# Near heads of the second attention: products moved to POOL, weighted values moved into the attention stage, a skew of two batches, the gates' softmax in two halves

## The reference

```
qk = x @ Wqk + bqk                      # x: layernorm of the residual
q, k = split(qk);  v = k                # 16 heads of 16
windows = [max(4, 256 // 2 ** h) for h in range(16)]
mask = (j <= i) & (j > i - windows[h])
att = softmax(where(mask, q @ k.T / sqrt(16), -inf))
out = att @ v
gates = softmax(x @ Wgate + bgate)      # over the 16 heads
y = (out * gates) @ Wproj + bproj
```

## Time and profile before

| | us |
|---|---|
| three timed runs, median | 1461.62 |
| lowest, highest of them | 1457.1, 1462.15 |
| profiled execution, its own time | 1458.09 |
| its span in the profile | 1456.4 |
| busy in the span: PE, DVE | 1237.8, 850.5 |
| busy in the span: ACT, POOL | 660.5, 666.6 |
| `project_local`, from PE's first product to the end of the last row | 529.30 to 636.30 |
| `project_local`, from there to its last instruction | 636.30 to 665.64 |
| `attend`, SP's first load to DVE's last instruction | 666.15 to 805.21 |

### The profile page before, as it was taken

How to read it: one execution, slowest core, us unless ns; L and a number is a source line. 1 busy time by engine, 2 the same in 40 slices (tenths; PEclk the granted TensorE clock), 3 DMA queues, 4 the chain that set the end, 5 groups by cost and what they waited for, 6 DMA issues and landing times. The chain is left out here.

```text
span 1456.4 us, 29479 instructions
## 1 busy us (share of the span) xinstructions
PE 1237.8 (85%) x9695; PEld 969.9 (67%) x9696; DVE 850.5 (58%) x1794; ACT 660.5 (45%) x1260; POOL 666.6 (46%) x616
## 2 busy tenths in 40 slices
PE   5886999999978959944998786798869999999996
PEld 3664555555547747732766666788847888878885
DVE  4897788888738849985554684433323333333332
ACT  2881666666755534420445552233213433333332
POOL 6865777776351304876000000454224554444553
PEclk9996899999999968775999998999979999999998
DMA  2487999999300025654442420000174334554331
GB/s 54 141 277 248 259 285 270 274 275 286 69 1 1 1 82 162 195 159 91 111 110 51 144 73 8 18 26 30 37 285 133 57 60 127 134 133 131 56 50 20
DMA packets 122865, 179.26 MB, mean 123 GB/s; under 512 B 26052, under 2 KB 83820, under 8 KB 122772
## 3 DMA queue, kind: packets, MB, share of 16 engines
q1 hardware_dynamic: 105876, 159.62, 37.6%
q0 software_dynamic: 16896, 18.44, 7.5%
HBM read 104.73 MB, written 74.31 MB: 123 GB/s over the span
## 5 line engine op out<-in xcount | busy, mean ns | idle before, releaser
L1635 DVE TENSOR_REDUCE att_top<-att_psS 128x4 f32<-128x512 f32 (+2 forms) x192 | 195.0, 1037 | 45.2 <-PE att_psS L1522 42.2
L2786 POOL DMA_INDIRECT out<-ffn1c_y,ffn1c_table x72 | 113.4, 1575 | 180.4 <-ACT ffn1c_y L2899 112.3
L2927 DVE TENSOR_TENSOR ffn1c_hid<-ffn1c_psG,ffn1c_sil 128x512 f32<-128x512 f32 x72 | 49.8, 692 | 145.6 <-PE ffn1c_psG L2827 145.6
L1606 ACT ACTIVATE att_prob<-att_psS 128x1024 f32<-128x1024 f32 (+1 forms) x96 | 83.3, 887 | 63.0 <-PE att_psS L1536 63.0
L1516 PE MATMUL att_psS<-pairs_ka,pairs_qa 48*128 48x384 f32 (+3 forms) x512 | 100.0, 399 | 11.8 <-DMA pairs_ka<-k_parts 7.2
L2827 PE MATMUL ffn1c_psG<-ffn1c_w_h,ffn1c_xh 128*128 x288 | 98.0, 422 | 11.1 <-DMA ffn1c_w_l<-experts_lo 6.0
L2435 POOL DMA_INDIRECT slots<-ffn1b_entry,ffn1b_sloti x64 | 62.9, 983 | 92.1 <-ACT ffn1b_act_h L2648 52.6
L1606 ACT ACTIVATE pairs_part<-att_psS 128x1024 f32<-128x1024 f32 (+1 forms) x96 | 83.0, 889 | 35.8 <-PE att_psS L1536 35.8
L2775 POOL DMA_INDIRECT ffn1c_rows<-normed_rows,ffn1c_table x72 | 71.2, 988 | 46.6 <-DVE ffn1c_gate L2947 22.9
L2827 PE MATMUL ffn1c_psG<-ffn1c_w_l,ffn1c_xh 128*128 x288 | 91.4, 399 | 0.0
L2827 PE MATMUL ffn1c_psG<-ffn1c_w_h,ffn1c_xl 128*128 x288 | 91.1, 398 | 0.0
(11 more groups left out here) (397 smaller groups left out, 3518.4 us busy)
## 6 DMA issues: line engine op xcount, KB each, us to landing
prep_raw<-in_w_all SPq DMA_DIRECT2D x27, 512.0 KB, 5.6
experts_hi<-ffn0w_room SPq DMA_DIRECT2D x27, 512.0 KB, 5.9
experts_lo<-prep_lo SPq DMA_DIRECT2D x27, 512.0 KB, 7.4
ffn1c_w_h<-experts_hi SPq DMA_DIRECT2D x8, 1536.0 KB
ffn1c_w_l<-experts_lo SPq DMA_DIRECT2D x8, 1536.0 KB
qkv_near<-near_keys SPq DMA_DIRECT2D x32, 320.0 KB, 4.3
q_parts<-pairs_part SPq DMA_DIRECT2D x8, 1024.0 KB
k_parts<-pairs_part SPq DMA_DIRECT2D x16, 512.0 KB
```

The lines of the kernel that those rows point to most:

```text
L1606: act.activation(dst, src, ACT.Exp, scale=0.25).then_inc(s["exp"], 1)
L1635: dve.tensor_reduce(dst, src, AX.X, ALU.max).then_inc(s["max"], 1)
L2786: pool.indirect_dma_start(out=rows_out, in_=y[:, t.buf, :], in_offset=None, out_offset=bass.IndirectOffsetOnAxis(ap=table[:, t.value:t.val ...
L2927: dve.tensor_tensor(hid[:, t.par, :], psG[:, t.par, 1, :], sil[:, t.par, :], ALU.mult).then_inc(s["act"], 1)
```

## The change

In `project_local`:
- `near_products` goes from DVE to POOL, ahead of `third_term` in POOL's loop; of the last batch POOL makes two of the four planes and DVE the other two (`last_products`). `near` has two buffers and `qkr` three.
- The near work of batch b-2 stands in iteration b (before: b-1). `turn_rows` and `high_rows`/`low_rows` run two batches ahead (before: one), so two batches are turned before the first product. PE's order in an iteration is products, gate logits, `turn_wide` of b-1, `turn_rows` of b+2.
- The gates' softmax is made for four batches at once, at two places of the loop, instead of once for each batch. The near shares are no longer multiplied with the gates here.
- `near_values` is gone from here. The shares of all batches stay in SBUF (`near_shares`) for the next block.

In `attend`:
- SP reads the shifted keys again (`near_in`, two transfers of 320 KB in each unit's stage), and POOL multiplies shares with gates, keys with that, and adds the planes (`near_values`), once for each batch, behind its bias addition.
- The four constants are written by POOL, and PE waits for them only ahead of its first psB product.

```diff
@@ project_local, SP
                 sp.wait_ge(s["rows"], 16 * (b + 1))
-                if b >= 3:
-                    sp.wait_ge(s["pv1"], b - 2)
+                if b >= 2:
+                    sp.wait_ge(s["prod"], b - 1)
                 for d in range(NW):
...
@@ project_local, PE
             turn_rows(0)
+            turn_rows(1)
             pe.wait_ge(s["wt"], len(ws))
-            for b in range(B):
-                products(b)
-                if b + 1 < B:
-                    turn_rows(b + 1)
-                gate_logits(b)
-                turn_wide(b)
+            for b in range(B + 1):
+                if b < B:
+                    products(b)
+                    gate_logits(b)
+                if b >= 1:
+                    turn_wide(b - 1)
+                if b + 2 < B:
+                    turn_rows(b + 2)
...
@@ project_local, ACT
             high_rows(0)
             normed(1)
+            high_rows(1)
+            normed(2)
             act.wait_ge(s["ones"], 2)
...
+            for b in range(B + 1):
+                if b == B // 2 + 1:
+                    gate_exp(0)
+                if b < B:
+                    values(b)
                 if b >= 1:
-                    near_exp(b - 1)
-                gate_exp(b)
-                second_term(b)
+                    first_term(b - 1)
                 if b + 2 < B:
-                    normed(b + 2)
+                    high_rows(b + 2)
+                if b >= 2:
+                    near_exp(b - 2)
+                if b >= 1:
+                    second_term(b - 1)
+                if b + 3 < B:
+                    normed(b + 3)
+            gate_exp(1)
             near_exp(B - 1)
...
@@ project_local, POOL
+            def near_products(b, planes):
+                pool.wait_ge(s["qs"], TG * (b + 1))
+                pool.wait_ge(s_near[b % 2], 16 * NW * (b // 2 + 1))
                 if b >= 1:
...
+                    pool.wait_ge(s["sc0"], b)
+                pool.tensor_tensor(prod[:, 0:planes], near[:, b % 2, 0:planes],
+                                   qkr[:, b % 3, :, PW:D].unsqueeze(1).to_broadcast([P, planes, TG, DW]),
+                                   ALU.mult).then_inc(s["prod"], 1)
 
             for b in range(B):
-                pool.wait_ge(s["prod"], b + 1)
+                near_products(b, NW if b + 1 < B else NW // 2)
                 third_term(b)
-                if b >= 1:
-                    near_values(b - 1)
...
@@ project_local, DVE
             low_rows(0)
+            low_rows(1)
...
-            for n in range(B + 1):
+            for n in range(B + 2):
+                if n == B // 2:
+                    gate_logits(0)
                 if n < B:
                     rows(n, (0, 1))
-                if n >= 1:
-                    near_products(n - 1)
+                if n == B + 1:
+                    last_products(B - 1)
+                if n >= 2:
+                    near_sums(n - 2)
                 if n < B:
                     rows(n, (2, 3))
-                if n >= 1:
-                    near_sums(n - 1)
-                if n + 1 < B:
-                    low_rows(n + 1)
-                if n >= 1:
-                    near_scores(n - 1)
-                if n < B:
-                    gate_logits(n)
-                    rests(n)
-                if n >= 1:
-                    near_shares(n - 1)
-                if n < B:
-                    gate_shares(n)
-            near_values(B - 1)
+                if n == B:
+                    gate_logits(1)
+                if 0 <= n - 1 < B:
+                    rests(n - 1)
+                if n >= 2:
+                    near_scores(n - 2)
+                if n + 2 < B:
+                    low_rows(n + 2)
+                if n >= 2:
+                    near_shares(n - 2)
+                if n == B // 2 + 1:
+                    gate_shares(0)
+                if n == B:
+                    gate_shares(1)
...
@@ attend, POOL
+            def near_values(b):
+                if b >= 1:
+                    pool.wait_ge(s["near1"], b)
+                pool.tensor_tensor(gated[:], pw[:, b], gates[:, TG * b:TG * (b + 1), PH:H].unsqueeze(1).to_broadcast(
+                    [P, NW, TG, DH]), ALU.mult).then_inc(s["gated"], 1)
+                pool.wait_ge(s["gated"], b + 1)
+                pool.wait_ge(s_near[b % 2], 16 * NW * (b // 2 + 1))
...
+            for n in range(4):
+                pool.memset(ka[KROWS:KROWS + MROWS, n], -1.0).then_inc(s["const"], 1)
+            pool.wait_ge(s["const"], 4)
...
@@ attend, SP
+            def near_in(u):
...
+                half = u.n // groups % 2
+                if u.after(2 * groups):
+                    sp.wait_ge(s["near1"], (u - 2 * groups).seq + 1)
+                for d in range(u.hg, NW, groups):
+                    rows = k_rows[bass.ds(u.seq, 1), NW - d:NW - d + S, :].rearrange("o (t p) c -> p (o t) c", p=P)
+                    sp.dma_start(near[:, half, d], rows).then_inc(s_near[half], 16)
...
                 values_in(u + 1)
+                near_in(u)
```

More of the change, by code:

```diff
@@ L747, in near_exp, with gate_exp @@
                 act.activation(sc, sc, ACT.Exp, scale=0.25).then_inc(s["sexp"], 1)
-            def gate_exp(b):
-                act.wait_ge(s["gl"], 3 * b + 3)
-                act.activation(glog, glog, ACT.Exp).then_inc(s["gexp"], 1)
+            def gate_exp(half):
+                act.wait_ge(s["gl"], 3 * half + 3)
+                part_of = gates[:, NT // 2 * half:NT // 2 * (half + 1), :]
+                act.activation(part_of, part_of, ACT.Exp).then_inc(s["gexp"], 1)
             def second_term(b):
@@ new lines, in gate_logits @@
+            def gate_logits(half):
+                at = slice(NT // 2 * half, NT // 2 * (half + 1))
+                shape = [P, NT // 2, H]
+                dve.wait_ge(s["gt"], B // 2 * (half + 1))
+                dve.tensor_tensor(gates[:, at, :], glog_ps[:, at, :], gb_sb[:].unsqueeze(1).to_broadcast(shape), ALU.add
+                                  ).then_inc(s["gl"], 1)
+                dve.wait_ge(s["gl"], 3 * half + 1)
+                dve.tensor_reduce(gmax[:, at], gates[:, at, :], AX.X, ALU.max).then_inc(s["gl"], 1)
+                dve.wait_ge(s["gl"], 3 * half + 2)
+                dve.tensor_tensor(gates[:, at, :], gates[:, at, :], gmax[:, at].unsqueeze(2).to_broadcast(shape), ALU.subtract
+                                  ).then_inc(s["gl"], 1)
@@ new lines, in gate_shares @@
+            def gate_shares(half):
+                at = slice(NT // 2 * half, NT // 2 * (half + 1))
+                dve.wait_ge(s["gexp"], half + 1)
+                dve.tensor_reduce(gsum[:, at], gates[:, at, :], AX.X, ALU.add).then_inc(s["gdone"], 1)
+                dve.wait_ge(s["gdone"], 3 * half + 1)
+                dve.reciprocal(gmax[:, at], gsum[:, at]).then_inc(s["gdone"], 1)
+                dve.wait_ge(s["gdone"], 3 * half + 2)
+                dve.tensor_tensor(gates[:, at, :], gates[:, at, :], gmax[:, at].unsqueeze(2).to_broadcast([P, NT // 2, H]),
+                                  ALU.mult).then_inc(s["gdone"], 1)
@@ L1114, in attend @@
         rec = k.sb("rec", [P, 2, TG, HG])
+        near = k.sb("near", [P, 2, NW, TG, DW])
+        pv = k.sb("pv", [P, NW, TG, DW])
+        gated = k.sb("gated", [P, NW, TG, DH])
         psA = k.ps("psA", [P, 2, 2, 512])
@@ L1196, in _ @@
         def _(pe):
-            pe.wait_ge(s["const"], 4)
             def query_tile(u, slot, t):
@@ L1241, in stage @@
                         if n == 0:
+                            if not v.after(1):
+                                pe.wait_ge(s["const"], 4)
                             pe.wait_ge(s["m_in"], 16 * v.value + 16)
@@ L1354, in stage @@
                                           ALU.mult).then_inc(s["norm"], 1)
-            for n in range(4):
-                dve.memset(ka[KROWS:KROWS + MROWS, n], -1.0).then_inc(s["const"], 1)
             walk(dve, stage, groups)
```

142 lines of the change are left out of this document (59 added, 83 removed).

## The result

The changed kernel takes 1466.72 us (median of 20 runs), the kernel before 1460.61 in 20 runs beside it: a ratio of 1.0038, with an interval of 1.0024 to 1.0052. It is slightly slower, where 1450 was forecast. In a later run the same pair gave 1449.2 against 1438.9, 1.0074 (1.0044 to 1.0104). The profiled execution took 1463.05 us and has a span of 1461.3, against 1458.1 and 1456.4 before.

A forecast was written before the change was run, and what follows sets the result against it. DVE was taken to set the pace in `project_local`, PE in `attend`. 1458.1 - 11.7 (`project_local`) + 2.5 (`attend`) = 1448.9, put at 1450 for the timed median; range 1442 to 1461, with under 1454.3 counted as faster.

The forecast's parts named there:

- the ring: In `project_local`, PE, ACT and DVE wait on one another in a cycle: 12.55 us, taken as 13.1 us a batch.
- (65.5 + 2.3) / 5: In `project_local`, 65.5 us for five batches at the cycle's pace, plus 2.3 for the first half of the gates' softmax.
- the forecast's 0.55: In `project_local`, us added to each batch's cycle for PE's lower clock, between bounds of 0 and 1.5.
- POOL's product: In `project_local`, the product moved to POOL takes 5.84 us and is ready before DVE wants it, with 4 us of cover.
- The start: In `project_local`, two sets of transposes ahead of the first product make the products start about 2.4 us later.
- The tail: End of `project_local`, from the last row on: 22.9 us against 29.3, 6.4 less.
- The whole block: All of `project_local`: 11.7 us less, with the later start, the shorter tail and waits on POOL counted.
- Waits between DVE and POOL: DVE operations with two SBUF inputs stand still behind POOL: in `attend` 1 us in all, between 0 and 10.
- an allowance of 2.5: In `project_local`, DVE's waits on POOL: 1.0 us at the first half's softmax and 1.5 in the tail, between 0 and 6.
- `attend`, the rest: SP's two new issues a unit cost at most 0.6 us each, stage 7.9; 2 us taken, 0.5 off for the constants.
- the rival "Slower": In `attend`, SP's queue becomes the bound: stage 9.0 us instead of 7.07, 31 us instead of 2, about 1479; chance 0.07.
- The sum: Whole kernel: 1458.1 - 11.7 + 2.5 = 1448.9 for an execution like the profiled one, forecast 1450.

## Why the prediction was wrong

**`project_local`, the ring: right in kind, a little short in size.** From the first product to the end of the last row 98.9 us, forecast 98.3. Single batches are uneven, 12.4 to 16.7 us between two `rests`, the mean of five 14.2 with the softmax of the first half in it; that is (65.5 + 2.3) / 5 = 13.6 in the forecast. So the five batches took 3 us more than I took, about as much was won elsewhere, and that the sum is so near is in part luck. The clock is 0.89 on average, but it did hold two of the five batches, one of which is the first of these stretches:

```profile
577.65:593.54 15.89, 12.85 (x66) 11.02 (x66) 10.82 (x18) 6.39 (x13) 11.12 (x3) 0.82 0.63 186
593.54:606.10 12.56, 11.61 (x69) 10.02 (x69) 9.25 (x14) 6.52 (x15) 6.33 (x2) 0.93 0.58 169
```

The other is the batch of 16.71 us, with a granted clock of 0.80. In these two PE's tiles 2 and 3 took 4.45 and 4.34 us, where they took 2.88 in the batch of 12.56; PE had stood idle for 3.04 and 3.90 us ahead of tile 2, and for 0.95 in the other. That is 3.0 us over five batches, 0.6 each, what the forecast's 0.55 allowed for. The gates' softmax stands in the same two batches.

**POOL's product: right.** 5.6 us, forecast 5.84, and DVE never waited for it.

**The start: right.** Products start 15.2 us after the last operation of the stage ahead, 12.95 before: 2.3 later, forecast 2.4.

**The tail: right**, 23.9 us, forecast 22.9. **The whole block**: 11.4 us less in the profiled pair, forecast 11.7. From the first product to SP's first load for `attend` the profiles of the three kernels with the old block have 135.9 to 136.9 us and the ten with the new one 122.6 to 126.2.

**Waits between DVE and POOL: right in size.** In `attend` 2.3 and 1.4 us for 11.5 and 7.4 us of waiting in these products (with the loads ahead of the store, and in the gap), each from two single profiles; forecast 1 with an end of 10. In `project_local` three of the gates' four operations with two inputs in SBUF were held up: the last product took 1.39 us where the subtraction of the same size and form took 0.42, in the first half the two took 0.88 and 0.72. That is 1.7 us in all, of an allowance of 2.5.

**"`attend`, the rest": this is the step that failed.** It said that the two issues cost at most 0.6 us each, "make it 7.9", with bounds of "0, and 0.8 a unit, 13 us", and took 2. The stage became 9.27 us. From the first to the last load of maxima there are 130.1 us where there were 110.4, 1.31 us a stage; the earlier start gives 2.1 back, which leaves 17.7. Two things in that step were wrong, and the experiments price both:

- I counted the near loads by their issues. The run with a quarter of the bytes shows that the issues with this quarter cost at most 4.1 us over twelve stages, and the other bytes 12.9. In the stage shown, 0.89 us came ahead of the store and 1.55 between store and landing; the step had nothing for the second.
- The mean busy share of 0.49 was held against it in the rival "Slower". But the load of the transfer engines comes in a burst between two waits of SP. A mean over such a stage says nothing about how long the last small transfer of the burst takes.

The mechanism stood there as the rival "Slower", with its stage of 9.0 us and a chance of 0.07, and it is what happened. Its price, 31 us, was too high: it compared with 7.07 us, two units of the earlier trace rows, where the mean of the stages before was 7.36 us (110.4 / 15), and it took the full amount in all 16, where the last two stages, with near loads but no more loads of scores, ran at 5.5 and 5.7 us. The stage that I read in parts (4.44 and 2.39 us) was also one in which SP had next to no time over; over all of `attend` it had waited 32.2 us for DVE, which hid part of the growth. So the forecast of 2 us, and its end of 13, were both under the 17.7 measured.

**The sum**, with what was measured: 1458.1 - 11.4 + 17.7 = 1464.4 for the profiled execution; it had 1463.05, with the 1.0 us late start in it and 2.6 us less in the blocks behind `attend`, for which the traces give no cause.

## What to carry to other kernels

When an engine issues a burst of transfers, then a small store whose landing it waits for before it issues more, bytes added to the burst can be on the path, however low the mean share of the transfer engines is; look at that share in slices of a quarter microsecond within one stage, and at the time from the small store to its landing. Put bulk transfers between the small store and its wait: here that alone turned 0.7% of loss into 0.4% of gain. Work that is moved to a later block takes its inputs with it: here 10 MB of loads cost 17.7 us where the block that gave the work away gained 11.4, until the loads were placed in the gap; the 5 us of `attend` that were left went when a part of the keys stayed in SBUF.

## What the runs showed of the hardware

- From the issue of the 6 KB store to SP's next load there were 1.3 us where SP had issued nothing for 6.4 us, and up to 4.9 us behind a unit's 1.4 MB from the same queue (kernel before with the loads; 4.6 in the changed kernel).
- Loads from ACT's queue in place of SP's still stretched SP's stage, to 8.54 us against 9.00 and 7.41, with 9.46 and 11.07 us in single stages. In it DVE's product was held up longer too, so not all of this need be the transfers.
- A DVE product of 12 columns with both inputs in SBUF took 170 ns where POOL was idle, and 0.6 to 1.8 us on average beside POOL's products, in the same place of the program; with one input in PSUM it took 171 ns beside the same POOL work.
- A POOL product of 2560 elements a partition took 5.64 us with the operand repeated over whole planes, and 4.56 us with it repeated over the 16 places of a head.
